# First pair of token blocks by eight plain products, the split of M's combinations during it, and h1T's product five matmuls later

## The reference

```python
x = x + einsum('bct,bcd->bdt', x, w0[adapter])                       # 64x64, mixes the tokens of one sequence
x = x + x @ W1 + (x @ A1[adapter]) @ B1[adapter]                     # rank 16
x = x + x @ W2.T + ((x @ A2[labeler]) @ B2.T) * 0.5                  # rank 32
logits = x @ Wr.T + 5 * one_hot(language)                            # 8 experts
gates = softmax over the two largest logits, 0 for the others
x = x + x @ W3.T + 2 * sum_e gates[e] * (x @ A3[e].T) @ B3[e]        # rank 16
```

## Time and profile before

| | us |
|---|---|
| median of 3 runs | 558.42 (558.06 to 558.95) |
| the profiled execution's own time | 558.88 |
| its span, first to last instruction | 557.1 |
| TensorE busy in it | 536.8 (96%) |
| VectorE, ScalarE, GpSimd busy | 251.1, 164.0, 167.1 |
| mean granted TensorE clock | 0.994 |

### The profile page before, as it was taken

How to read it: one execution, slowest core, us unless ns; L and a number is a source line. 1 busy time by engine, 2 the same in 40 slices (tenths; PEclk the granted TensorE clock), 3 DMA queues, 4 the chain that set the end, 5 groups by cost and what they waited for, 6 DMA issues and landing times.

```text
span 557.1 us, 9123 instructions
## 1 busy us (share of the span) xinstructions
PE 536.8 (96%) x2801; PEld 475.3 (85%) x2801; DVE 251.1 (45%) x615; ACT 164.0 (29%) x319; POOL 167.1 (30%) x251
## 2 busy tenths in 40 slices
PE   7999999999999999999787999999999999999997
PEld 7999999999999999999666788787887878878785
DVE  3851312132311112117597464654756546565463
ACT  5641311121111111117342332333323333233322
POOL 2501000000000002338872444434444344443400
PEclk9999999999999999999898999999999999999999
DMA  8803020045150101020140321323213233132402
GB/s 292 294 3 127 2 75 15 1 165 169 61 176 35 26 29 35 32 80 1 28 157 2 126 98 54 91 77 125 96 53 92 76 125 96 53 92 76 126 16 76
DMA packets 24059, 46.74 MB, mean 84 GB/s; under 512 B 7636, under 2 KB 13396, under 8 KB 23908
## 3 DMA queue, kind: packets, MB, share of 16 engines
q1 hardware_dynamic: 23844, 45.85, 25.0%
q0 software_dynamic: 192, 0.59, 0.3%
HBM read 33.39 MB, written 13.04 MB: 83 GB/s over the span
## 4 chain that ended last, share of the span: by engine, by line
PE 75%; SPq 5%; DVE 5%; issue 5%; POOL 4%; DMA 4%; ACT 1%; POOLq 1%; DVEq 0%; ACTq 0%
PE bank L1274 23%; PE bank L1308 19%; PE bank L1225 15%; PE bank L1294 6%; PE bank L1241 4%; DMA b1s<-b1scr 3%; PE bank L1356 3%; SPq L411 2%; SPq L427 2%; PE bank L1364 2%; DMA w2raw<-in_w_dram 1%; DVE xb_lo L893 1%; DVE ost L1107 1%; ACT xb_hi L760 1%; POOL bd_hi L524 1%
## 5 line engine op out<-in xcount | busy, mean ns | idle before, releaser
L1274 PE MATMUL bank<-e_lo,w1t_hi 128*128 128x488 f32 (+2 forms) x240 | 86.9, 362 | 0.0
L1274 PE MATMUL bank<-e_hi,w1t_hi 128*128 128x488 f32 (+2 forms) x240 | 86.8, 362 | 0.0
L1274 PE MATMUL bank<-e_hi,w1t_lo 128*128 128x488 f32 (+2 forms) x240 | 86.7, 361 | 0.0
L893 DVE TENSOR_TENSOR w1t_lo<-raw,w1t_hi 128x1024 fp32r<-128x1024 f32 x18 | 23.5, 1303 | 69.8 <-ACT w1t_hi L654 60.0
L1225 PE MATMUL bank<-g_hi,w2s_hi 128*128 128x384 f32 (+1 forms) x144 | 48.3, 336 | 0.3 <-DVE e_lo L893 0.3
L1274 PEld LDWEIGHTS bank<-e_lo,w1t_hi 128*128 128x128 f32 x240 | 45.1, 188 | 3.9
L1274 PEld LDWEIGHTS bank<-e_hi,w1t_hi 128*128 128x128 f32 x240 | 45.0, 188 | 4.0
L1274 PEld LDWEIGHTS bank<-e_hi,w1t_lo 128*128 128x128 f32 x240 | 45.1, 188 | 3.9
L1225 PE MATMUL bank<-g_lo,w2s_hi 128*128 128x384 f32 (+1 forms) x144 | 48.2, 335 | 0.0
L1225 PE MATMUL bank<-g_hi,w2s_lo 128*128 128x384 f32 (+1 forms) x144 | 48.2, 335 | 0.0
L893 DVE TENSOR_TENSOR e_lo<-bank,e_hi 128x384 fp32r<-128x384 f32 (+1 forms) x24 | 13.0, 559 | 60.7 <-ACT e_hi L689 60.7
(11 more groups left out here) (210 smaller groups left out, 1329.8 us busy)
## 6 DMA issues: line engine op xcount, KB each, us to landing
raw<-in_x_dram SPq DMA_DIRECT2D x16, 512.0 KB, 3.5
out_dram<-ost SPq DMA_DIRECT2D x32, 256.0 KB, 2.1
b1s<-b1scr SPq DMA_DIRECT2D x32, 217.5 KB, 2.7
raw<-in_b1w_dram SPq DMA_DIRECT2D x10, 512.0 KB, 3.4
w2raw<-in_w_dram SPq DMA_DIRECT2D x7, 512.0 KB, 7.8
graw<-in_w3a3wr_dram SPq DMA_DIRECT2D x4, 768.0 KB, 8.8
graw<-in_w3a3wr_dram SPq DMA_DIRECT2D x8, 196.0 KB, 7.0
b1scr<-b1stage_hi SPq DMA_DIRECT2D x8, 192.0 KB
```

The lines of the kernel that those rows point to most:

```text
L893: V.tensor_tensor(dst, src, f32(hi), ALU.subtract).then_inc(signal, 1)
L1274: ins = nc.tensor.matmul(stage_bank(u, j)[:, 0:WIDTH[c]], W1T[u][a][:, k, :], EX[c][z][:, k, :], start=(k == 0 and (a, z) == TERMS[0]), st ...
```

## The change

Pair 0 is computed with M's four blocks as they are: eight products, 96 matmuls, no left sums and no adds (`group`; banks 0 to 3 hold the four results). A single matmul that stood ahead of it (L1473) is gone. `b12` gets a hi and lo part. ScalarE and VectorE split b11, b12, b21, b22 at the end of M's rows, and t1 to t3 while pair 0 is computed, t4 at its end. The x of pair 0 is split as it is, block 1 into `CS` and `DS`. `sum0` and the GpSimd sums of pair 0 are gone. GpSimd forms the `BD` parts (`diagonal`) of blocks 0 and 1 ahead of the row before the last instead of behind all rows. ScalarE splits the x of pair 1 (`left_hi(1)`) ahead of `exp_of(0)` and `xn_hi(1)`. Pair 1 stands out of TensorE's loop, with waits for t1 to t4; the loop runs over pairs 2 to 6. In every later pair `h1_into` of the first block stands five matmuls later, and the small steps behind it move too. SP reads the four indices of `load_b1s` ahead of its wait for the tile.

```diff
@@ sync @@
-            def load_b1s(b, s):
-                for h in range(PER):
-                    a = index(idx_a, PER * b + h, NA)
-                    lab = index(idx_l, PER * b + h, NL)
+            def rows_of(b):
+                return [(index(idx_a, PER * b + h, NA), index(idx_l, PER * b + h, NL)) for h in range(PER)]
+            def load_b1s(chosen, s):
+                for h, (a, lab) in enumerate(chosen):
...
-                    sp.wait_ge(s_sum, 4 * p + 4)
-                    sp.wait_ge(s_opl, OPS * p + 5)
+                    if isinstance(p, int) and p == 0:
+                        sp.wait_ge(s_pl, 3)
...
                     if n % 2 and not last:
+                        chosen = rows_of(2 * p + 2 + s)
                         done = held(sp, 4 * p + n + 1)
                         sp.wait_ge(s_idx, 48)
                         sp.wait_ge(s_y, done)
-                        load_b1s(2 * p + 2 + s, s)
+                        load_b1s(chosen, s)
@@ gpsimd @@
             for k in range(K - 1):
+                if k == K - 2:
+                    diagonal(0, 0, 0)
+                    diagonal(1, 1, 0)
                 row_there(k)
...
-            nc.gpsimd.tensor_tensor(sum0[:, :, :], r21, r22, ALU.add).then_inc(s_sum, 1)
-            diagonal(0, 0, 0)
-            diagonal(1, 1, 0)
             chosen = choose(0)
...
             take(0, chosen)
-            pool.wait_ge(s_raw[0], 16 * (ROWS // 2 + 1))
-            pool.wait_ge(s_opl, 2)
-            nc.gpsimd.tensor_tensor(sum0[:, :, :], sum0[:, :, :], r11, ALU.subtract).then_inc(s_sum, 1)
             pool.wait_ge(s_acc, ACC_A + ACC_B)
-            pool.wait_ge(s_sum, 2)
-            nc.gpsimd.tensor_tensor(tmp[:, :, :], r12, sum0[:, :, :], ALU.subtract).then_inc(s_sum, 1)
             nc.gpsimd.memset(f32(b1s[0][:, D + C3:]), 0.0).then_inc(s_b1z, 1)
...
@@ scalar, first_pair_hi @@
+                plain_hi(CS[0][:, :, :], raw[1][:, 0:KH, :])
+                plain_hi(DS[0][:, :, :], raw[1][:, KH:K, :])
                 act.wait_ge(s_tr, formed(1, KH - 1))
                 split_hi("t1", WHOLE)
                 act.wait_ge(s_b2st, 16 * 3)
                 xn_hi(0, YB)
+                act.wait_ge(s_tr, formed(4, KH - 2))
+                act.wait_ge(s_trd, 3)
+                split_hi("t2", WHOLE)
                 h1_t(0, 0)
+                split_hi("t3", WHOLE)
                 h2_t(0, 0)
+                left_hi(1)
+                exp_of(0)
                 xn_hi(1, YB)
@@ vector, first_pair_lo @@
                 first_low_rank(0, 0, steps)
-                split_lo("t3", FRONT, SPLIT_HI["t3a"])
+                split_lo("t1", WHOLE, SPLIT_HI["t1"])
                 second_low_rank(0, 0, steps)
+                split_lo("t2", WHOLE, SPLIT_HI["t2"])
+                route(0, 0, steps)
+                left_lo(1)
                 xn_lo(1, YB)
+                gates(0, 0, steps)
                 first_low_rank(1, 1, steps)
-                split_lo("t4", WHOLE, SPLIT_HI["t4"])
-                route(0, 0, steps)
-                sum_p7(0)
-                gates(0, 0, steps)
+                split_lo("t3", WHOLE, SPLIT_HI["t3"])
                 second_low_rank(1, 1, steps)
@@ vector, pair_lo @@
-                gates(b0, 0, steps)
                 sum_p1(p)
+                operand_lo(CS[1][:, :, :], raw[1][:, 0:KH, :], CS[0][:, :, :], ops + 5)
                 sum_p5(p)
                 xn_lo(b1, YB)
+                gates(b0, 0, steps)
...
@@ tensor, first_pair_products @@
+                group(a11, "b11", 0, 0, 12, True)
+                group(a11, "b12", 1, 0, 9, True)
+                group(a11, "b12", 1, 9, 12, True)
+                narrow(0, first_block, YB)
+                group(a12, "b21", 0, 0, 6, False)
                 mixed(0, 0)
+                group(a12, "b21", 0, 6, 9, False)
+                group(a12, "b21", 0, 9, 12, False).then_inc(s_pw, 1)
                 h1_across(0, 0)
+                group(a12, "b22", 1, 0, 5, False)
                 h1_into(0, 0, 0)
+                group(a12, "b22", 1, 5, 9, False)
+                group(a12, "b22", 1, 9, 12, False).then_inc(s_pw, 1)
+                group(a21, "b11", 2, 0, 6, True)
                 h2_across(0, 0)
+                group(a21, "b11", 2, 6, 12, True)
                 h2_into(0, 0)
+                narrow(1, second_block, YB)
+                group(a21, "b12", 3, 0, 8, True)
                 mixed(1, 1)
...
+                group(a22, "b22", 3, 11, 12, False).then_inc(s_pw, 1)
@@ tensor, pair_products @@
-                part("p5", 0, 4)
+                part("p5", 0, 9)
                 h1_into(b0, 0, p)
-                part("p5", 4, 11)
-                h2_across(b0, 0)
-                part("p5", 11, 12)
+                part("p5", 9, 12)
                 part("p6", 0, 4)
+                h2_across(b0, 0)
+                part("p6", 4, 10)
                 h2_into(b0, 0)
-                part("p6", 4, 12)
+                part("p6", 10, 12)
                 narrow(b1, second_block, YB)
-                part("p2", 0, 9)
+                part("p2", 0, 7)
                 mixed(b1, 1)
-                part("p2", 9, 12)
-                gated_across(b0, 0)
-                part("p7", 0, 3)
+                part("p2", 7, 12)
+                part("p7", 0, 5)
+                gated_across(b0, 0)
+                part("p7", 5, 9)
                 h1_across(b1, 1)
-                part("p7", 3, 8)
+                part("p7", 9, 12)
+                part("p3", 0, 1)
                 h1_into(b1, 1, p)
-                part("p7", 8, 12)
-                part("p3", 0, 3)
+                part("p3", 1, 8)
                 h2_across(b1, 1)
-                part("p3", 3, 9)
+                part("p3", 8, 12)
+                part("p4", 0, 2)
                 h2_into(b1, 1)
-                part("p3", 9, 12)
-                part("p4", 0, 12)
+                part("p4", 2, 12)
```

More of the change, by code:

```diff
@@ L784, in first_pair_hi @@
                 split_hi("b11", WHOLE)
+                split_hi("b12", WHOLE)
+                rows_raw(ROWS - 1, 1, [1])
+                act.wait_ge(s_rd, 3 * LAST + 1)
+                nc.scalar.activation(S[0][:, :, 0:C3], TBC[:, :, :], ACT.Copy).then_inc(s_s0h, 1)
+                act.wait_ge(s_ra, 4 * LAST)
+                act.wait_ge(s_rd, 3 * LAST)
+                split_hi("b21", FRONT)
+                rows_raw(ROWS - 1, 1, [2])
+                split_hi("b22", FRONT)
+                act.wait_ge(s_ra, 4 * LAST + 4)
@@ L1113, in first_pair_lo @@
             def first_pair_lo(steps):
-                left_lo(0)
+                plain_lo(XA[1][:, :, :], raw[0][:, :, :], XA[0][:, :, :], 1)
                 rows_raw(ROWS - 1, 1)
@@ L1202, in pair_lo @@
                 ght_lo(b1, 1)
-                last_tiles_lo(p)
-            r21 = raw[1][:, 0:KH, :]
+                xm_lo(0, bank[BC], 4 * p + 3)
+                xm_lo(1, bank[BB], 4 * p + 4)
+                ost_odd(p, 1)
+                ost_odd(p, 3)
             first_pair_lo(Steps(0, 0))
@@ L1293, in narrow @@
                     for a, z in TERMS:
-                        ins = nc.tensor.matmul(bank[to][:, 0:SC], left[a][:, k, :], S[z][:, k, :], start=(k == 0 and (a, z) == TERMS[0]),
+                        ins = nc.tensor.matmul(bank[to][:, 0:SC], left(a, k), S[z][:, k, :], start=(k == 0 and (a, z) == TERMS[0]),
                                                stop=(k == K - 1 and (a, z) == TERMS[-1]), skip_group_check=True)
@@ L1365, in tile, with group @@
                 ins.then_inc(s_y, 1)
+            def group(left, name, to, lo_, hi_, opens):
+                right = MO[name]
+                for n in range(lo_, hi_):
+                    k, (a, z) = n // 3, TERMS[n % 3]
+                    ins = nc.tensor.matmul(bank[to][:, :], left(a, k), right[z][:, k, :], start=(opens and n == 0),
+                                           stop=(not opens and n == 3 * KH - 1), skip_group_check=True)
+                return ins
             def first_pair_products():
@@ L1394, in first_pair_products @@
+                pe.wait_ge(s_pl, 3)
                 pe.wait_ge(s_b2s, 16)
                 h2_into(0, 0)
-                pe.wait_ge(s_add, 2)
-                pe.wait_ge(s_opl, 5)
-                there("t3b")
-                part("p7", 0, 6)
+                narrow(1, second_block, YB)
+                group(a21, "b12", 3, 0, 8, True)
                 mixed(1, 1)
-                part("p7", 6, 12)
-                pe.wait_ge(s_opl, 6)
-                there("b22")
+                group(a21, "b12", 3, 8, 12, True).then_inc(s_pw, 1)
@@ L1404, in first_pair_products @@
+                group(a22, "b21", 2, 0, 4, False)
                 h1_across(1, 1)
-                part("p3", 0, 6)
+                group(a22, "b21", 2, 4, 9, False)
                 h1_into(1, 1, 0)
-                part("p3", 6, 12)
-                pe.wait_ge(s_add, 3)
-                there("t4")
```

(20 more changed lines are left out.)

294 lines of the change are left out of this document (140 added, 154 removed).

## The result

The changed kernel took 549.01 us (median of 4 runs, 547.88 to 549.34) beside 558.68 us (558.06 to 559.37) for the kernel before on the same chip: ratio 0.9823, 95% interval 0.9804 to 0.9843. The profiled execution took 548.72 us, its span is 546.9. 548.6 had been forecast, within 543.0 to 553.5.

The account below looks back on a forecast made before the run. TensorE, busy 96% of the span, was taken as the bound, so gains come from its waits. Pair 0's 4.5 us and pairs 1 to 7's 5.4 us sum to 9.9 us, giving 548.6 us, range 543.0 to 553.5.

Parts of the forecast that it names:

- Waits of pair 0 gone, 11 matmuls more: Pair 0: waits of 3.54, 4.63 and 1.05 us and 3.4 us of slow clock go, 2.5 us added: 39.6 us.
- take(0): GpSimd in pair 0: runs from 258.0 to 265.9, held by VectorE's operations, feeding narrow(0) with 0.8 us to spare.
- rival C: Pair 0: take(0) ends later than 266.7, narrow(0) waits again with its slow clock: 551.5 us; chance 0.10.
- The new wait: Pair 0, mixed(1,1): TensorE waits 3.9 us for xn_lo, queued behind pair 1's x, plus 1.7 us of half clock.
- Rival B: Pair 0: x comes in time, 543.0 us, or early enough that the clock stays up, 545.3; chance 0.27.
- Pair 0 in sum: Pair 0: 39.6 + 3.9 + 1.7 = 45.2 us instead of 49.7, a gain of 4.5 us.
- Pairs 1 to 7: Pairs 1 to 7: 6.3 us of waits gone less 0.9 us in the last pair, a gain of 5.4 us.
- 6.3 us, all gone: Pairs 1 to 7, h1_into: standing 1.15 us later removes all waits for b1s, if b1s lands as now.
- rival E: Each pair: xb_hi waits for the output store and the second narrow waits, slower than before, 560.5 us; chance 0.03.
- rival D: Pairs 1 to 7: b1s lands later for SP's new reading order, waits stay: 554.9 us, half of it 551.8; chance 0.10.
- The last pair's gh: Last pair, gated_across: waits 1.1 us instead of 0.24, 0.9 us lost.

Follow-up runs that it names:

- e2: Changed kernel with SP loading pair 1's x ahead of the two w0 blocks in pair 0: 543.37 us, ratio 0.9725.
- e8: Changed kernel with six of VectorE's two-input operations beside take(0) replaced by memsets, their results left out: 545.78 us, one execution.
- e4: Changed kernel with the orders of TensorE, VectorE and ScalarE in pairs 1 to 7 as before: 554.62 us, ratio 0.9912.
- e11: Changed kernel with VectorE's gates(b0) again ahead of sum_p1, sum_p5 and xn_lo(b1) in pairs 1 to 7: 557.89 us, ratio 0.9978.
- e9: Kernel before with only the new orders of TensorE, VectorE and ScalarE in pairs 1 to 7: 554.12 us, ratio 0.9918.
- e10: Kernel before with only the first block's steps moved in pairs 1 to 7, h1_into five matmuls later: 559.87 us, ratio 1.0016.
- e12: Kernel before with the first block's steps moved, VectorE's new order and gated_across(b0) moved, second block's other steps as before: 559.81 us, ratio 1.0015.
- e5: Changed kernel with SP's reading of the four indices put back to the order before in pairs 0 to 6: 547.90 us, ratio 0.9806.
- e1: Changed kernel with the splits of pair 1's x behind xn_hi(1) on ScalarE and second_low_rank(1,1) on VectorE: 544.56 us, ratio 0.9744.
- e3: Changed kernel with SP loading pair 1's x between the two w0 blocks: 545.30 us, ratio 0.9755.

## Why the prediction came out

The time was right to 0.4 us. In pair 0 it was right for the reason given; in pairs 1 to 7 the size was right for a reason that doesn't hold alone, which is luck.

- **Waits of pair 0 gone, 11 matmuls more.** Without a wait 39.6 us had been summed up; 39.76 were measured (e2).
- **take(0).** It was to last 7.9 us, from 258.0 to 265.9. It lasted 7.4, from 258.77 to 266.15. A start 0.8 us later and a length 0.5 us shorter nearly cancelled. `narrow(0)` starts at 267.25 without a wait, 1.1 us behind take(0)'s end, so rival C didn't come. e8 shows the cause as it was told, VectorE's two-input operations, for 2.7 us. The Trainium skill's rule (GPSIMD Engine Reference, section Specifications) that GpSimd contends for SBUF with VectorE's instructions of two SBUF inputs is borne out here, 3.21 against 1.44 us for the same two subtractions.
- **The new wait.** 14.7 us from the memset to the issue of x: 14.6. Landing 3.4: 3.55 to the start of the split. Wait 3.9 by starts: 287.26 less 283.34 and one matmul is 3.7. left_lo took 1.42 rather than 1.23 us. The terms given for xn_lo, 284.2 + 1.06 + 1.23 + 0.40 + 0.3, make 287.2 and not 286.9, and xn_lo ended at 287.12; TensorE came 0.6 us later than forecast, so two errors nearly cancel in the wait. The half clock behind it 1.7: 1.7 by the rows of this profile; in e4's and e11's, with 6.8 us at half clock, pair 0 was 0.9 and 1.2 us longer. Rival B (x in time) came only where e2 made it come, and its price held: 543.0 forecast without a wait, 543.37 measured.
- **Pair 0 in sum.** 45.2 forecast, 44.83 measured; gain 4.5 forecast, 4.9 measured, 4.6 by e4.
- **Pairs 1 to 7.** 5.4 us forecast; 5.8 in the profiles, 4.8 by e9. The period is the 34.0 us forecast. (The rows that the prediction calls pair 3 in the earlier trace rows lie in pair 4, those of the earlier trace rows in pair 3; that changes nothing in its sums.) But the step "6.3 us, all gone" because the product stands 1.15 us later fails as a reason: e10 has that and gains nothing. The prediction left out where TensorE's regained time goes. TensorE comes 0.8 us sooner to `mixed` of the second block, and nothing makes xn_lo as much sooner; it had VectorE's new order and the later place of the second block's steps at no price and no worth, and without them the gain is gone (e11: 1.2 us of the whole left; e12: none). The chain that holds xn_lo is the one that rival E starts from, `xb_hi` behind the output store; there it was followed only to the second `narrow`. The trace of the kernel before had the rows that show how little room there was, first VectorE's, then TensorE's in pair 3:

```profile
395.56 0.39 DVE L893 TENSOR_TENSOR xn_lo<-bank,xn_hi 128x232 fp32r<-128x232 f32 x1
...
396.13 0.31 PE L1318 MATMUL bank<-xn_hi,bd_hi 128*128 128x232 f32 x1
```

xn_lo ends at 395.95 and is used at 396.13, so of the 0.82 us that the wait for b1s cost, TensorE could gain no more than 0.2 there.
- **b1s lands later, by the order of the readings** (rival D): no. e5 shows no difference.
- **The last pair's gh.** 1.1 us of waiting forecast, 0.83 measured.
- **Rival E** (the output store): no `narrow` waits in pairs 1 to 7.

## What to carry to other kernels

A transfer that stands ahead of a step in an engine's queue delays it even where the two have nothing to do with each other: e1 swaps the two on the engines, e2 lets the transfer be asked for ahead of ones that nobody waits for yet, and they won 3.8 and 4.9 us more. When a wait is taken away, the engine that waited comes sooner to its next steps: look up for each of them how long its operand had been ready, and follow the operand's own chain over the other engines, since with slack of some tenths of a microsecond the wait comes up again at the next step (b1s, then xn_lo, then h1c); such an edit is worth testing in parts, because the part that it is named after may gain nothing alone.

## What the runs showed of the hardware

- Two waits of TensorE of 0.75 and 1.06 us, 3.5 us apart, left the granted clock at 1.00 (e3); one of 3.54 us was followed by 3.4 us at about half, as after the waits of 3.39 and 4.48 us before. The same wait of 3.54 us had 6.8 us at half clock in e4's profile, begun 1.5 us before the wait ended, and pair 0 was 0.9 us longer.
- A pair of GpSimd subtractions of 128x256 took 1.44 us with VectorE filling memory beside it (e8) and 3.21 us with VectorE's two-input operations (the changed kernel). VectorE's gm took 0.49 us there and 1.10 us in e3, where GpSimd's subtractions ran beside it.
- The start of pair 0 varies by 1.6 us between executions (260.48 to 262.06 in the profiles of the changed kernel timed again and of e11), with nothing changed ahead of it; comparing stretches from pair 0 on is sharper than comparing spans.
